# Expert loop of a decoder layer: the second layer's bias product reads 128 rows in place of three

## The chip, the cores and the metric

The kernel runs on one core of a Trainium2 chip. The metric is the device time of one execution in microseconds; the time given is the median of several runs. The engines of the core are named as the profile names them: PE is TensorE (PEld its weight loads), DVE is VectorE, ACT is ScalarE, POOL is GpSimd, SP is SyncE, which here only issues DMAs.

## What is computed

A decoder layer on x of 64 sequences x 64 tokens x 128 features: causal self-attention, cross-attention on a context, and a feed-forward layer with 8 experts of which each token takes 2. Each is followed by a residual sum and a layer norm. The change is in the experts:

```python
scores = x @ Wr.T + br                       # 8 experts
_, idx = top_k(scores + biases_N, 2)         # two experts per token
h = einsum('md,ndh->nmh', x, Wl1) + bl1      # first layer, 128 -> 512
a, b = h[..., :256], h[..., 256:]
y = einsum('nmh,nhd->nmd', silu(a) * b, Wl2) + bl2   # second layer, 256 -> 128
out = sum over the token's two experts of weight * y
```

The bias of the second layer, bl2 (8 x 128), is what the changed product adds.

## The kernel before

The 4096 tokens stand as 32 tiles of 128. The self-attention and the cross-attention are software pipelines over these tiles. In the cross-attention each group of four tiles is also routed: its tokens are sent by indirect DMA (`send`, POOL, L622) to per-expert regions of a DRAM buffer `xbuf`. The expert loop then works on 71 row tiles, each of 128 rows of one expert (`J` in the code). Its first tiles are interleaved with the last of the cross-attention; the last group is routed inside the loop.

Engines run their own instruction streams in a fixed order and meet by semaphores. `slot_tile(i, q)` is one step of the loop on each engine. On PE it does, in this order:

- `layer1(i)`: L1813, four fp32 products of 128 x 128 (two records each in the profile, so 8), `w_now` (the expert's first-layer weights) against the transposed rows `xT`
- `layer2(i - 2)`: L1823, two fp32 products (4 records), `gT` against `wl2_sb`, into columns 0 to 127 of a bank of PSUM, and then the bias product, L1825, which closes the same accumulation
- `x_T_slot(i + 2)`: L1803, the transposition of a coming row tile

SP fetches the rows (L443, 65 KB, from `xbuf`) and the weights (L448, 256 KB) four and three steps ahead; the fetch of weights waits until the first layer four tiles earlier is done. ACT copies the transposed rows (L878), copies and scales the result (L894) and applies silu (L886). DVE makes `gT` (L1440). POOL puts the result by indirect DMA into `zbuf` (`put`, L632).

The bias is added by PE. `b2_part` holds it split into three bf16 parts, one to a row (`split_b2`, DVE, six steps in the cross-attention); `ones_b`, a 128 x 128 matrix of ones in bf16, is the stationary operand, of which L1825 uses three rows. Summing the three rows gives the bias in every row of the result. The expert's number is read from a register (`bass.ds(e, 1)`), as for `wl2_sb`.

POOL writes the constants at the start (L479 to L521), some of them behind the first two tiles' L477, then issues five DMAs (L523 to L527), and next works on L533 of the first tile.

Of the kernel before, what the change touches and what calls it, by code (L numbers as in the profile page):

```python
# [25 lines left out]
BF16 = mybir.dt.bfloat16  # L26
# [5 lines left out]
P = 128  # L32
D = 128
# [10 lines left out]
def later(t, n):  # L44

    return t >= n if isinstance(t, int) else True


def decoder(nc, x, ctxT, g1, wqT, wkvT, woutT, g2, xwq, xwk, xwvT, xwo, bo, wrT, br, wl1, bl1, wl2, bl2, bN, out, xbuf, zbuf):
# [3 lines left out]
    NE = wrT.shape[1]  # L53
# [22 lines left out]
    with ctx:  # L76
        def sb(name, shape, dt=F32):
            return ctx.enter_context(nc.sbuf_tensor(name, shape, dt))
# [4 lines left out]
        bank = [ctx.enter_context(nc.psum_tensor(f"bank{i}", [P, 512], F32)) for i in range(8)]  # L83
# [34 lines left out]
        wl2_sb = sb("wl2_sb", [P, NE, NH, D])  # L118
        b2_sb = early[0:3, 0:W]
        b2_up = early[0:3, W:W + W // 2].bitcast(BF16)  # L120
        b2_part = sb("b2_part", [3, NE, D], BF16)
        part = sb("part", [3, 3])

        X = sb("X", [P, T, D])
# [44 lines left out]
        tri_b, ones_b = sb("tri_b", [P, P], BF16), sb("ones_b", [P, P], BF16)  # L169
# [169 lines left out]
        def numbers(eng_type, table, most, t, known):  # L339

            n = min(EB, J - t)
            _, values = nc.values_load_multi_w_load_instructions(
                table[0:1, t:t + n], engines=[eng_type], min_val=0, max_val=most,
                skip_runtime_bounds_check_because="an expert is a count of NE - 1 bounds, a row a block within the buckets")
            for k in range(n):
                known[t + k] = values[k]
# [63 lines left out]
        def _(sp):  # L410
# [5 lines left out]
            for n, (src, rows, _, _) in enumerate(slices):  # L416
                if n >= SELF_SPLITS:
                    sp.wait_ge(split, 2 * n)
                sp.dma_start(staging(n), src).then_inc(staged, 16)
                if n == 1:  # L420
                    sp.dma_start(wout_sb[:, :, :], woutT).then_inc(w_out, 16)
                    sp.dma_start(g2_sb[:, :], g2.partition_broadcast(P)).then_inc(w_out, 16)
                    sp.dma_start(X[:, 4:T, :], x_v[:, 4:T, :]).then_inc(x_rest, 16)
# [50 lines left out]
        def _(pool):  # L474
# [29 lines left out]
            ln_in(1, 1)  # L504
            nc.gpsimd.memset(tri_b[:, :], 1.0).then_inc(consts, 1)
            nc.gpsimd.memset(ones_b[:, :], 1.0)
            nc.gpsimd.memset(blank[:, 0:D], 0)
            nc.gpsimd.memset(blank[:, D + 1:ROW], 0)
            nc.gpsimd.memset(blank[:, D:D + 1], NOWHERE).then_inc(consts, 1)
# [408 lines left out]
        def _(dve):  # L918
# [5 lines left out]
            def split_slice(n):  # L924
                _, rows, hi, lo = slices[n]
                dve.wait_ge(staged, 16 * max(n + 1, SELF_SPLITS))
                V.tensor_copy(hi, staging(n)).then_inc(split, 1)
                dve.wait_ge(split, 2 * n + 1)
                V.tensor_tensor(lo, staging(n), hi.bitcast(F32), ALU.subtract).then_inc(split, 1)
# [213 lines left out]
            def cross(i, p):  # L1143
# [45 lines left out]
                if 2 <= i < 2 + 6:  # L1189
                    split_b2(i - 2)  # L1190
# [9 lines left out]
                            iota8[:, :].unsqueeze(1).broadcast_to([P, NE, NE]), ALU.is_ge)  # L1200

            def split_b2(n):
                out_of = b2_part[:, :, :].rearrange("r n d -> r (n d)")
                if n == 0:
                    dve.wait_ge(w_ffn, 80)
                    V.tensor_copy(b2_up[:, :], b2_sb[:, :]).then_inc(f["b2"], 1)
                if n == 1:
                    dve.wait_ge(f["b2"], 1)
                    V.tensor_scalar(out_of, b2_up[:, :], part[:, 0:1], None, ALU.mult).then_inc(f["b2"], 1)
                if n == 2:  # L1210
                    dve.wait_ge(f["b2"], 2)
                    V.tensor_tensor(b2_sb[:, :], b2_sb[:, :], b2_up[:, :], ALU.subtract).then_inc(f["b2"], 1)
                if n == 3:
                    dve.wait_ge(f["b2"], 3)
                    V.tensor_copy(b2_up[:, :], b2_sb[:, :]).then_inc(f["b2"], 1)
                if n == 4:
                    dve.wait_ge(f["b2"], 4)
                    V.scalar_tensor_tensor(out=out_of, in0=b2_up[:, :], scalar=part[:, 1:2], in1=out_of, op0=ALU.mult,
                                           op1=ALU.add)
                    V.tensor_tensor(b2_sb[:, :], b2_sb[:, :], b2_up[:, :], ALU.subtract).then_inc(f["b2"], 1)  # L1220
                if n == 5:
                    dve.wait_ge(f["b2"], 5)
                    V.scalar_tensor_tensor(out=out_of, in0=b2_sb[:, :], scalar=part[:, 2:3], in1=out_of, op0=ALU.mult,
                                           op1=ALU.add).then_inc(f["b2"], 1)
# [279 lines left out]
        def _(pe):  # L1504
            M = nc.tensor.matmul
# [311 lines left out]
            def layer2(t, q):  # L1817
                pe.wait_ge(hs["gT"], t + 1)
                if later(t, 2):
                    pe.wait_ge(hs["yb"], t - 1)  # L1820
                e = known[t]
                for c in range(NH):
                    M(bank[6 + q % 2][:, 0:D], gT[:, q % 2, c * P:(c + 1) * P],  # L1823
                          wl2_sb[:, bass.ds(e, 1), c, :].rearrange("h n d -> h (n d)"), start=(c == 0), stop=False)
                M(bank[6 + q % 2][:, 0:D], ones_b[0:3, :], b2_part[:, bass.ds(e, 1), :].rearrange("r n d -> r (n d)"),  # L1825
                  start=False, stop=True).then_inc(hs["L2"], 1)

            known = {}
# [1 line left out]
            def slot_tile(i, q):  # L1830
                of_tile(layer1, i, q, 0)
                if i == -1:
                    pe.wait_ge(f["tableA"], TABLE_A)
                if (i + 1) % EB == 0 and 0 <= i + 1 < J:
                    expert_numbers(mybir.EngineType.PE, i + 1, known)
                of_tile(layer2, i, q, 2)
                of_tile(x_T_slot, i, q, -2)
                if i == 4:
                    route_T(G - 1)
                if i == 6:  # L1840
                    route_scores(G - 1)
                if i == 12:
                    route_places(G - 1)
# [71 lines left out]
```

## Time and profile before

| | us |
|---|---|
| median of 3 runs (843.33 to 844.18) | 843.4 |
| span of the profiled execution | 876.8 |
| self-attention, cross-attention | 0 to about 692 |
| expert loop, first half (with sends) | about 692 to 782 |
| expert loop, second half | about 782 to 846 |
| last sums, layer norm, output | about 846 to 877 |

The profiled execution is 33.4 us longer than the median of the timed runs. Times below are from the start of its span. Over the whole span PE is busy 91%, its weight loads 75%, DVE 71%, ACT 68%, POOL 52%. A busy PE is not a PE at its peak, since its products overlap and their ends are modelled; what counts for pace is the distance between starts.

### The profile page before, as it was taken

What the parts mean: (1) busy time and instruction counts of PE and PEld (TensorE: products, weight loads), DVE (VectorE), ACT (ScalarE), POOL (GpSimd) and SP (SyncE); (2) the same over time, 40 slices, a digit from 0 to 9 for tenths busy, and PEclk for the clock granted to TensorE, in tenths of its full rate; (3) what the DMA queues carried; (4) which work ended last, traced back from release to release, by engine and by line L of the source; (5) the groups of instructions that cost most, each with busy time, mean ns of one, the idle gap of its engine ahead of it and who ended that gap; (6) DMA issues with size and microseconds to landing.
All of it is one profiled execution on the core that took longest, in us unless ns stands there. A gap on an engine that the chain in (4) does not pass through costs nothing.

```text
span 876.8 us, 26473 instructions
## 1 busy us (share of the span) xinstructions
PE 797.6 (91%) x9276; PEld 659.0 (75%) x9308; DVE 621.1 (71%) x1834; ACT 593.9 (68%) x1444; POOL 453.7 (52%) x441
## 2 busy tenths in 40 slices
PE   3799999999999988999999999999998979879996
PEld 2577787878777767887888888878786867768862
DVE  4877887878788757898787878878788534334425
ACT  2677888888788756677777767767675555446535
POOL 5477676776767732222535353535343455555543
PEclk9899999999999999999999999999999898999998
DMA  8499999000000000000000000000000445557636
GB/s 259 86 154 161 155 157 126 1 0 0 0 0 0 2 1 7 7 7 7 24 13 22 15 22 16 22 15 19 19 19 28 147 144 173 180 168 218 205 126 232
DMA packets 69392, 64.79 MB, mean 74 GB/s; under 512 B 5702, under 2 KB 54985, under 8 KB 69168
## 3 DMA queue, kind: packets, MB, share of 16 engines
q1 hardware_dynamic: 62592, 51.42, 29.0%
q0 software_dynamic: 4624, 9.61, 3.2%
q10 hardware_dynamic: 2080, 2.49, 0.9%
q8 instruction: 59, 0.97, 0.5%
q14 instruction: 37, 0.30, 0.1%
HBM read 35.37 MB, written 28.58 MB: 73 GB/s over the span
## 4 chain that ended last, share of the span: by engine, by line
PE 52%; issue 18%; POOL 12%; DVE 8%; ACT 5%; DMA 2%; another core or an unknown queue 2%; POOLq 0%; SPq 0%; ACTq 0%; DVEq 0%
PE bank L1813 8%; PE bank L1709 7%; PE bank L1509 5%; POOL rq L533 5%; PE bank L1511 5%; PE bank L1510 5%; PE bank L1823 3%; POOL PR L538 3%; PE bank L1684 3%; PE bank L1697 3%; PE bank L1585 2%; PE bank L1803 2%; PE bank L1593 2%; ACT VBD L393 2%
## 5 line engine op out<-in xcount | busy, mean ns | idle before, releaser
L393 ACT COPY VBD<-bank 64x512 f32<-64x512 f32 x192 | 111.3, 580 | 28.3 <-PE bank L1511 25.5
L570 POOL TENSOR_TENSOR PR<-PR,rL 128x1024 f32<-128x1024 f32 x32 | 60.9, 1904 | 115.0 <-DVE rL L1119 114.8
L533 POOL TENSOR_TENSOR rq<-ssq,mhalf 128x17 f32<-128x17 f32 x32 | 99.3, 3102 | 15.6 <-DVE ssq L968 15.1
L632 POOL DMA_INDIRECT zbuf<-PT,KT x71 | 69.7, 982 | 65.7 <-ACT PT L894 32.4
L538 POOL TENSOR_TENSOR PR<-PR,rL 128x1024 f32<-128x1024 f32 x32 | 61.0, 1906 | 82.4 <-DVE rL L999 82.4
L1440 DVE SCALAR_TENSOR_TENSOR stage<-bank,b_now,early 128x128 f32<-128x128 f32 x142 | 43.3, 347 | 77.1 <-ACT early L886 42.5
L1813 PE MATMUL bank<-xT,w_now 128*128 128x128 f32 x568 | 82.0, 291 | 1.1
L622 POOL DMA_INDIRECT xbuf<-xg,slot x64 | 65.2, 1018 | 34.1 <-DVE xg L1314 21.6
L886 ACT ACTIVATE early<-bank,b_now 128x128 f32<-128x128 f32 x142 | 44.7, 368 | 52.5 <-PE bank L1813 37.9
L1813 PEld LDWEIGHTS bank<-xT,w_now 128*128 128x128 f32 x568 | 77.1, 209 | 3.3 <-issue 3.2
L802 ACT ACTIVATE PT<-bank 128x512 f32<-128x512 f32 x64 | 38.3, 600 | 43.5 <-PE bank L1697 41.7
L1709 PE MATMUL bank<-VBD,PT 128*64 128x128 f32 x1024 | 64.7, 280 | 3.0 <-ACT PT L802 3.0
L1709 PEld LDWEIGHTS bank<-VBD,PT 128*64 128x64 f32 x1024 | 56.8, 139 | 11.6 <-ACT PT L802 9.5
L1593 PE MATMUL bank<-arena 128*128 128x128 f32 x512 | 62.8, 275 | 1.9 <-issue 1.1
L1585 PE MATMUL bank<-PT,VBD 128*128 128x512 f32 x128 | 63.4, 618 | 0.0
L1593 PEld LDWEIGHTS bank<-arena 128*128 128x128 f32 x512 | 59.8, 192 | 2.9 <-ACT arena L728 1.6
L1106 DVE TENSOR_REDUCE mx<-bank 128x8 f32<-128x512 f32 x64 | 43.8, 684 | 25.3 <-PE bank L1684 25.2
L575 POOL TENSOR_TENSOR rs<-ve,mhalf 128x1 f32<-128x1 f32 x32 | 18.6, 581 | 74.3 <-DVE ve L1134 73.9
L1509 PE MATMUL bank<-vo_lo,cT_hi 96*128 96x512 f32 x128 | 54.8, 428 | 2.4 <-DVE VBD L393 1.5
L712 ACT ACTIVATE PR<-bank 128x512 f32<-128x512 f32 x64 | 34.7, 595 | 28.9 <-PE bank L1563 28.9
L1511 PE MATMUL bank<-vo_hi,cT_hi 96*128 96x512 f32 x128 | 50.4, 394 | 0.0
L1510 PE MATMUL bank<-vo_hi,cT_lo 96*128 96x512 f32 x128 | 50.4, 393 | 0.0
(252 smaller groups left out, 2312.6 us busy)
## 6 DMA issues: line engine op xcount, KB each, us to landing
w_now<-in_wl SPq DMA_DIRECT2D x71, 256.0 KB
xbuf<-blank SPq DMA_DIRECT2D x1, 17160.0 KB, 119.6
KT<-xbuf SPq DMA_DIRECT2D x71, 65.0 KB
VBD<-zbuf SPq DMA_DIRECT2D x4, 512.0 KB, 5.0
out<-X SPq DMA_DIRECT2D x8, 256.0 KB, 2.3
cT<-in_ctxT ACTq DMA_DIRECT2D x16, 96.0 KB, 1.9
zbuf<-PT,KT POOLq DMA_INDIRECT x71
wl_sb<-in_wl POOLq DMA_DIRECT2D x1, 1024.0 KB, 9.2
```

Of the source, the lines that this page charges most:

```text
L393: u = copy(VBD[h * SEQ:(h + 1) * SEQ, p, s, lo:lo + blocks, :], bank[CHUNK_BANK[c]][s * SEQ:(s + 1) * SEQ, :].rearrange("k (a d) -> k a d" ...
L533: nc.gpsimd.tensor_tensor(rq[:, :], ssq[:, :], mhalf[:, 0:HEADS + 1], ALU.pow).then_inc(a["pow"], 1)
L538: nc.gpsimd.tensor_tensor(v, v, rL[:, p, :].unsqueeze(2).broadcast_to([P, HEADS, SEQ]), ALU.mult)\
L622: nc.gpsimd.indirect_dma_start(out=xbuf, out_offset=at, in_=xg[:, k, tt, :], in_offset=None)\
L632: nc.gpsimd.indirect_dma_start(out=zbuf, out_offset=at, in_=yb[:, t % YB, :], in_offset=None, bounds_check=K2 * TOK - 1, oob_is_err=False) ...
L1509: M(out_, l_hi, r_lo, start=True, stop=False)
L1510: M(out_, l_lo, r_hi, start=False, stop=False)
L1511: return M(out_, l_hi, r_hi, start=False, stop=True)
L1585: M(bank[4 + s][:, :], VBD[:, p, s, 0, :], PT[:, s * HW:(s + 1) * HW], start=True, stop=True)\
L1593: m = M(bank[0][:, 0:D], OT[:, k, :], wout_sb[:, k, :], start=(k == 0), stop=(k == NBLK - 1))
L1709: m = M(bank[bk][s * SEQ:(s + 1) * SEQ, 0:D], PT[:, k * P + s * SEQ:k * P + (s + 1) * SEQ], VBD[:, p, s, k, :], start=(k == 0), stop=(k == ...
L1813: m = M(bank[2 + q % 2][:, c * P:(c + 1) * P], w_now[:, q, c * P:(c + 1) * P], xT[:, q % 2, :], start=True, stop=True)
```

## The change

`b2_part` gets 128 rows in place of three. POOL fills it with zeros once among the constants, DVE writes the three parts into its first three rows as before, and the bias product reads all 128 rows of it and all 128 rows of `ones_b`. The tile has the same number of bytes in each partition as before. Lines behind L506 stand one lower in the changed kernel.

```diff
-        b2_part = sb("b2_part", [3, NE, D], BF16)
+        b2_part = sb("b2_part", [P, NE, D], BF16)
...
             nc.gpsimd.memset(ones_b[:, :], 1.0)
+            nc.gpsimd.memset(b2_part[:, :, :], 0.0)
             nc.gpsimd.memset(blank[:, 0:D], 0)
...
             def split_b2(n):
-                out_of = b2_part[:, :, :].rearrange("r n d -> r (n d)")
+                out_of = b2_part[0:3, :, :].rearrange("r n d -> r (n d)")
...
-                M(bank[6 + q % 2][:, 0:D], ones_b[0:3, :], b2_part[:, bass.ds(e, 1), :].rearrange("r n d -> r (n d)"),
+                M(bank[6 + q % 2][:, 0:D], ones_b[:, :], b2_part[:, bass.ds(e, 1), :].rearrange("r n d -> r (n d)"),
                   start=False, stop=True).then_inc(hs["L2"], 1)
```

## Rows read from the trace of the kernel before

**Rows 1.** The page's head: span and instructions.

```profile
span 876.8 us, 26473 instructions
```

**Rows 2.** Stretches: from:to, length, busy us (instructions) by engine, granted clock, DMA share, GB/s.

```profile
0.00:22.00 22.00, 7.92 (x46) 6.39 (x47) 9.32 (x25) 6.27 (x15) 12.60 (x37) 0.98 0.82 258
692.00:782.00 90.00, 73.59 (x508) 64.13 (x508) 35.34 (x155) 41.86 (x144) 48.49 (x51) 0.91 0.52 157
782.00:800.00 18.00, 18.00 (x144) 16.13 (x144) 7.98 (x31) 11.66 (x41) 9.28 (x10) 0.99 0.76 233
782.00:846.00 64.00, 62.24 (x485) 54.86 (x484) 27.33 (x103) 39.29 (x137) 33.69 (x35) 1.00 0.64 196
```

**Rows 3.** The chain of work that ended last, 692 to 847 us, shares by line.

```profile
by line: PE bank L1813 43.9%; PE bank L1823 17.2%; PE bank L1803 10.6%; another core or an unknown queue 8.4%; PE bank L1825 5.6%; issue 5.1%; ACT early L886 3.0%; DVE stage L1440 2.4%; ACT xT L878 1.3%; ACT PT L894 1.0%; POOL zbuf L632 0.6
```

**Rows 4.** Timeline of PE, 787.8 to 790.8 us: start, length, line, operands, rows*columns, count.

```profile
788.36 0.61 PE L1823 MATMUL bank<-wl_sb,stage 128*128 x4
788.90 0.23 PE L1825 MATMUL bank<-b_part,ones_b 3*128 x1
789.06 0.33 PE L1803 MATMUL bank<-ident,KT 128*128 128x128 f32 x1
789.23 1.06 PE L1813 MATMUL bank<-xT,w_now 128*128 128x128 f32 x8
790.12 0.61 PE L1823 MATMUL bank<-wl_sb,stage 128*128 x4
790.66 0.22 PE L1825 MATMUL bank<-b_part,ones_b 3*128 x1
```

**Rows 5.** Weight loads by line, 782 to 816 us: busy us, mean ns | idle before.

```profile
L1813 PEld LDWEIGHTS bank<-xT,w_now 128*128 128x128 f32 x152 | 19.8, 201 | 0.0
L1823 PEld LDWEIGHTS bank<-wl_sb,stage 128*128 128x128 f32 x76 | 10.0, 192 | 0.0
L1803 PEld LDWEIGHTS bank<-ident,KT 128*128 128x128 f32 x19 | 2.6, 139 | 1.5 <-issue 0.3
L1825 PEld LDWEIGHTS bank<-b_part,ones_b 3*128 3x128 bf16 x19 | 1.7, 91 | 2.3
```

**Rows 6.** Timeline of PE near 43 us: fp32 transpositions one behind another.

```profile
43.13 1.04 PE L1542 MATMUL bank<-ident,arena 128*128 128x128 f32 x8
44.00 0.27 PE L1548 MATMUL bank<-ident,kn 128*128 128x128 f32 x1
```

**Rows 7.** Timeline of weight loads near 46 us: fp32, then bf16.

```profile
46.01 0.86 PEld L1577 LDWEIGHTS bank<-ident,PR 128*128 128x128 f32 x8
46.83 0.21 PEld L1558 LDWEIGHTS bank<-causal,ident_b 128*128 128x128 bf16 x2
```

**Rows 8.** Timeline of weight loads near 392 us: the first of 64 rows.

```profile
391.97 0.15 PEld L1684 LDWEIGHTS bank<-KT,QT 64*64 64x64 f32 x4 [0.17 <-issue]
```

**Rows 9.** Timeline of PE near 415 us: short bf16 products of 128 rows.

```profile
414.94 0.22 PE L1739 MATMUL bank<-picked,ones_b 128*128 128x24 bf16 x3
415.02 0.18 PE L1741 MATMUL bank<-before,ones_b 128*128 128x32 bf16 x1
```

**Rows 10.** L1825 in 692 to 782, then 782 to 847 us: ns min/median/max, first and last start.

```profile
L1825 PE MATMUL bank<-b_part,ones_b x35: 224/225/283, 693.3 to 781.6; 3*128 x35
...
L1825 PE MATMUL bank<-b_part,ones_b x36: 224/225/225, 783.6 to 845.9; 3*128 x36
```

**Rows 11.** Timeline of POOL in the first 17 us.

```profile
1.12 0.53 POOL L482 MEMSET causal<- 128x512 bf16 x1
...
16.45 3.10 POOL L533 TENSOR_TENSOR rq<-ssq,mhalf 128x17 f32<-128x17 f32 x1 [4.47 <-DVE ssq L968]
```

**Rows 12.** POOL by line, 692 to 782 us; then what SP waited for, 782 to 846 us.

```profile
L632 POOL DMA_INDIRECT zbuf<-PT,KT x34 | 33.5, 986 | 34.5 <-ACT PT L894 22.5 <-issue 10.3 <-DVE xg L1314 1.6
L622 POOL DMA_INDIRECT xbuf<-xg,slot x15 | 14.8, 988 | 4.3 <-issue 4.3
...
SPq L448 <- PE bank L1813: 7.5, 16, 1.3
```

## The prediction

> **What bounds the kernel now.** I read the stages first, then the chain of work, then one tile at full pace, then its idle gaps. The expert loop does 71 row tiles (a row tile: 128 gathered tokens of one expert). It begins near 692 us and ends near 846 us of a span of 876.8 us [rows 1, 2]. In 782 to 846 us PE is busy 62.24 of 64 us, DVE 27.33, ACT 39.29, POOL 33.69, and the DMA engines 64% [rows 2]; in 782 to 800 us PE has no free time at all (18.00 of 18.00). The chain over the whole loop is mostly PE's: L1813, L1823, L1803 and L1825 (the changed product) together hold 43.9 + 17.2 + 10.6 + 5.6 = 77.3% [rows 3]. So a shorter PE tile should shorten the end. Before 782 us this is weaker: 35 products of L1825 take 90 us there, PE is busy 73.59 of it, and its granted clock averages 0.91.
>
> One tile at full pace is in [rows 4]: L1823 starts at 788.36, L1825 at 788.90, L1803 (the transposition of a coming tile's rows) at 789.06, L1813 (the first layer) at 789.23, and L1823 again at 790.12 us. That is a period of 1.76 us: 0.54 + 0.16 + 0.17 + 0.89. Eight products of L1813 take 0.89, so one fp32 step is 0.11. Three such steps are 0.33 of the 0.54, and the last step, from L1823 into L1825, is then **0.21, not 0.11**. Three of the fifteen steps stand out: into L1825 (0.21), out of it (0.16), and the one after L1803 (0.17).
>
> The weight loads show the same from the other side [rows 5]. In 34 us at full pace, loads of L1813 and L1823 have 0.0 us of idle ahead of them: each is made while the product before it still runs. The load of L1825 has 2.3 us over 19 (0.12 each) and that of L1803 1.5 us over 19 (0.08 each). These two are the ones at which the count of rows changes, from 128 to 3 and back to 128.
>
> **What the change does to a tile.** It replaces 71 products of 3 rows by 71 of 128 rows, in the same place, of the same 128 columns; the sum is the same, since the added rows are zero. No product is added, no wait is added or taken away.
>
> Is the number of rows what costs, or the bf16 type, or the register address of the expert? Other places tell. (a) A bf16 product of 128 rows right after fp32 products of 128 rows: the two loads of L1558 follow those of L1577 with no idle ahead of them; the last of L1577's begins near 46.87 - 0.14 = 46.73 (0.139 is the length of such a load in [rows 5]), L1558's first at 46.83, a normal step of 0.10 [rows 7]. Type alone costs nothing. (b) From fp32 products of 128 rows to fp32 products of 64 rows, no type change: L1684's load has 0.17 us of idle [rows 8]. Rows alone cost. (c) bf16 products of 128 rows and few columns follow each other at (415.02 - 414.94) / 3 = 0.03 us [rows 9]: such a load is short. (d) The register address is also on L1823, whose loads have no idle [rows 5].
>
> The Trainium skill says the same in "TensorEngine Tiling (Array Packing)", Key Properties: changing the tiling mode drains the engine, and a contraction over 32 rows or fewer is one of its row modes. It gives no figure; the sum does not use it.
>
> - Into L1825: 0.21 becomes one fp32 step, 0.11. **0.10 saved**; no lower end of the step below 0.11 is in sight, since the fp32 product before it must stream.
> - Out of L1825: 0.16. Its stream of 128 bf16 columns hides L1803's fp32 load or is hidden by it. The load paces at 0.11, as the transpositions of L1542 do: (44.00 - 43.13) / 8 = 0.109 [rows 6]; the floor is the short bf16 step of (c), 0.03. I take 0.11, the nearer row, since the next load is the same kind as L1542's. **0.05 saved** (ends 0 and 0.13).
> - After L1803: 0.17. The first load behind the switch is not hidden, so the next product is late; without the switch it is a step of L1542, 0.109. **0.06 saved** (ends 0 and 0.06).
>
> The sum is 0.10 + 0.05 + 0.06, with rounding of the rows about **0.20 us a tile**: 1.76 becomes 1.56. Ends: 0.10 if only the way in is gained, 0.29 if the way out falls to 0.03.
>
> **How many tiles gain.** After 782 us 36 of the products stand [rows 10] in 64 us: 1.78 each, practically all at PE's pace. They give 36 x 0.20 = 7.2 us. Before 782 us there are 35 [rows 10]; by the starts of L1825 in the timeline, from 693.3 to 781.6 us, 18 of their 34 intervals are 1.76; the rest end in waits on ACT, DVE or DMA that a faster PE does not shorten. They give 18 x 0.20 = 3.6 us. Together 10.8 us. If all 71 gain it is 14.2.
>
> What is late next in each part? Before 782 us it may be POOL: 34 puts (L632) and 15 sends (L622) there, each 0.99 us and, by L622's own row (4.3 us over 15), 0.29 of issue [rows 12]: 49 x 1.28 = 62.7 us, against 35 x 1.56 = 54.6 of PE. That holds the head's gain down to about what I count. After 782 us POOL has 35 x 1.28 = 45 us for 56. The DMA engines go from 76% at 233 GB/s (782 to 800 us) to 0.76 x 1.76 / 1.56 = 86%; the busiest stretch of the trace, the first 22 us, has 82% at 258 GB/s [rows 2]. This is close. SP still waits 7.5 us for L1813 in 782 to 846 us before it may fetch weights [rows 12], so these fetches are held by PE and not by bandwidth.
>
> **The rest.** One memset on POOL, of 128 x 1024 bf16. L482 writes half as much in 0.53 [rows 11], so it costs 1.0 us at about 7.5 us. POOL is then idle 4.47 us ahead of L533 at 16.45 us, and that idle covers it; the DMAs that POOL issues in between start 1 us later, all for data of later stages. Cost 0; uncovered it would be +1.0. DVE still writes three rows.
>
> **Own time.** The sum was made in an execution whose span, 876.8 us, is 33.4 us over the median of 843.4. Part of this must be waits that the timed runs don't have, and if they lie in the loop, more tiles run at PE's pace: that pulls towards 14.2. I take the count of the trace: 843.4 - 10.8 = **832.6 us**.
>
> **Rivals.**
> - **DMA or ACT takes over after 782 us.** With a period that can't fall below 1.66, the tail gives 3.6 and all gives 7.2: 836.2 us. For it: 86% DMA share. Against it: SP's waits for PE.
> - **Only the way in is gained** (the 0.16 and 0.17 belong to L1803's transposition): 54 x 0.10 = 5.4, 838.0 us. For it: L1803 is itself a different kind of step. Against it: L1542 is too, and runs at 0.109.
> - **Nothing is gained.** If a load can pass a running product only when it uses other rows of the array, a 128-row load behind a 128-row product has to wait as the 3-row load does, and the time stays at 843.4. Against it: loads of L1813 and L1823, all 128 rows behind 128 rows, have 0.0 idle [rows 5].
>  The Trainium skill states that rule ("TensorE: Matmul & The Clock Gate", Part 3, Measured speedup vs the span model: LDWEIGHTS overlaps an in-flight MATMUL only when its row group differs); the trace disagrees with it here.
> - **Slower.** The load of L1803 may no longer begin while L1825 runs. Now it begins 0.16 after L1825's start though that product lasts 0.23 (0.225) us [rows 4, 10], over 128 rows of which L1825 holds three. If a 128-row L1825 keeps those rows until its end, the way out goes from 0.16 to 0.23, and if the way in stays at 0.21, this is +0.07 x 71 = 5.0: 848.4 us. It decides from the point at which that load's wait costs more than the way in saves. Against it: bf16 products of 128 rows follow each other at 0.03 though each lasts 0.17 [rows 9].
>
> **How the numbers follow.** Forecast (0.20 a tile, 47 to 71 tiles, 829 to 834.5): 0.60. More than that (way out at 0.03): 0.05, down to 823 (71 x 0.29). DMA or ACT takes over: 0.12. Way in only: 0.09. Nothing: 0.10. Slower: 0.04. The range 829.0 to 839.0 holds the first and the two partial cases, 0.81, and leaves out the rest. A measurement of this kernel can tell about 0.2% from no change, 1.7 us. Faster by more: 0.60 + 0.05 + 0.12 + 0.09 = 0.86; within it 0.10; slower 0.04.
>
> **What would show it.** In the profile after: the load of L1825 (there L1826, one line lower) with no idle ahead of it, likewise L1803's; the period at 1.56 in the stretch that now has 1.76; PE's share of the chain still near 77%. The prediction is wrong if the period stays at 1.76 (nothing gained), if it is 1.66 (way in only), or if it falls to 1.56 in single tiles while new waits of PE for a DMA or for ACT stand between them. A granted clock below 0.91 over the first half of the loop would mean that PE's longer pauses cost back what its shorter tiles gave.

## The result

| | before | changed |
|---|---|---|
| median of 9 runs, us | 843.8 | 841.4 |
| lowest, highest | 841.7, 846.2 | 839.4, 843.1 |
| ratio, 95% interval | 1 | 0.9955 (0.9938 to 0.9972) |

The change makes the kernel faster by 0.45% (2.4 us by the medians, 3.8 by the ratio), where 10.8 us were forecast, and the time lies above the range of 829 to 839. The direction was right, and so was what the prediction said of PE's tile; two thirds of the forecast gain did not arrive (by the medians, more than three quarters).

PE's tile did become shorter, and by more than forecast. This is PE's timeline of the changed kernel in a stretch at full pace (start, length, line, operands, rows*columns, count; lines stand one lower than in [rows 4]):

```profile
764.43 0.61 PE L1824 MATMUL bank<-wl_sb,stage 128*128 x4
764.87 0.22 PE L1826 MATMUL bank<-b_part,ones_b 128*128 x1
764.93 0.28 PE L1804 MATMUL bank<-ident,KT 128*128 128x128 f32 x1
765.05 1.06 PE L1814 MATMUL bank<-xT,w_now 128*128 128x128 f32 x8
765.94 0.61 PE L1824 MATMUL bank<-wl_sb,stage 128*128 x4
```

The period is 765.94 - 764.43 = 1.51 us, where [rows 4] has 1.76. From L1824's start to the bias product: 0.44 (was 0.54), so that step is now 0.11. Out of the bias product: 0.06 (was 0.16). After the transposition: 0.12 (was 0.17). The sum of the three is 0.25 us a tile. The weight loads of the changed kernel in 765 to 808 us (the view of [rows 5]) show why:

```profile
L1814 PEld LDWEIGHTS bank<-xT,w_now 128*128 128x128 f32 x216 | 26.4, 192 | 1.1 <-ACT xT L879 1.1
L1824 PEld LDWEIGHTS bank<-wl_sb,stage 128*128 128x128 f32 x112 | 14.7, 192 | 0.5 <-issue 0.5
L1804 PEld LDWEIGHTS bank<-ident,KT 128*128 128x128 f32 x26 | 3.7, 142 | 0.3
L1826 PEld LDWEIGHTS bank<-b_part,ones_b 128*128 128x128 bf16 x27 | 2.7, 100 | 0.0
```

The load of the bias product has no idle ahead of it any more (2.3 us over 19 before) and the transposition's 0.3 over 26 (1.5 over 19). At 0.25 a tile, 71 tiles would give 17 us. So the question is where most of it went.

One thing has to be put right first. The execution of the kernel before on which the prediction rests had a span of 876.8 us, 33 above the median. The profiled execution of the changed kernel has a span of 840.2 (841.96 us in all), and another of the kernel before, from the first experiment, has 845.3. Comparisons below use these two. In the one of 845.3 the 71 bias products take 126.4 us, in place of 152.6 in the one that the prediction read: the many waits before 782 us belong to that one execution and not to the kernel.

### The profile page after: what moved, and what is told of

Same layout as the page of the kernel before. It is cut to its first block, busy times and chain, and to the rows that moved or that the text cites. A ratio compares the mean times of both kernels' runs of the same rounds, so it can differ in the third digit from the quotient of the medians.

```text
span 840.2 us, 26506 instructions
## 1 busy us (share of the span) xinstructions
PE 773.7 (92%) x9308; PEld 648.0 (77%) x9308; DVE 620.4 (74%) x1834; ACT 596.3 (71%) x1444; POOL 453.9 (54%) x442
## 4 chain that ended last, share of the span: by engine, by line
PE 40%; issue 22%; POOL 17%; DVE 9%; ACT 6%; DMA 4%; SPq 1%; POOLq 0%; ACTq 0%; DVEq 0%
POOL rq L534 7%; PE bank L1710 6%; PE bank L1814 5%; PE bank L1510 5%; PE bank L1512 4%; PE bank L1511 4%; POOL PR L539 3%; PE bank L1824 2%; PE bank L1698 2%; ACT VBD L393 2%; PE bank L1685 2%; POOL rs L548 2%; POOL rs L544 2%; POOL rs L477 2%; PE bank L1586 1%
## 5 line engine op out<-in xcount | busy, mean ns | idle before, releaser
L534 POOL TENSOR_TENSOR rq<-ssq,mhalf 128x17 f32<-128x17 f32 x32 | 99.2, 3101 | 16.9 <-DVE ssq L969 16.4
L623 POOL DMA_INDIRECT xbuf<-xg,slot x64 | 64.8, 1012 | 34.0 <-DVE xg L1315 21.4
L1814 PE MATMUL bank<-xT,w_now 128*128 128x128 f32 x568 | 78.1, 282 | 4.1 <-DMA w_now<-in_wl 2.7
L1814 PEld LDWEIGHTS bank<-xT,w_now 128*128 128x128 f32 x568 | 71.0, 196 | 6.0 <-ACT xT L879 3.2
L969 DVE TENSOR_REDUCE ssq<-arena 128x17 f32<-128x1088 f32 x32 | 41.2, 1288 | 12.9 <-ACT arena L677 5.2
```

Source lines behind the costliest of these rows:

```text
L534: nc.gpsimd.tensor_tensor(rq[:, :], ssq[:, :], mhalf[:, 0:HEADS + 1], ALU.pow).then_inc(a["pow"], 1)
L623: nc.gpsimd.indirect_dma_start(out=xbuf, out_offset=at, in_=xg[:, k, tt, :], in_offset=None)\
L1814: m = M(bank[2 + q % 2][:, c * P:(c + 1) * P], w_now[:, q, c * P:(c + 1) * P], xT[:, q % 2, :], start=True, stop=True)
```

## The experiments

All tables below count from the start of the loop's first bias product, and call the loop what lies between it and the last bias product, since the loop's own start moves by some 5 us from one execution to the next (682 to 688 us). The last send is the start of POOL's last L622 (L623). "Fetch of tile 40" is the DMA of the rows of row tile 40 (L443; tiles are counted from 0). It is the first tile that depends on the last group's routing: SP issues its fetch only when all sends have landed (L435).

### 1. The kernel before and the changed one again

> The kernel before, unchanged, for an execution whose span is near its timed median. Theory Q (the queue of POOL caps the first half of the expert loop): SP fetches the rows of tile 40 (L443 behind L435) only after POOL's last send, and POOL's indirect DMAs stand 1.28 us apart with no wait for the last ten or so before it; that fetch is issued about as long after the loop's first product of L1825 as in the changed kernel, where it is 750.97 - 686.31 = 64.7 us, within 1 us. Rival P (PE sets the first half as well): it is issued about 40 x 0.245 = 8 to 10 us later relative to that product, 73 to 75 us. Period of a tile at full pace 1.757 us in both.

> The changed kernel, unchanged. Period at full pace 1.512 us (steps of 0.112, 0.056 and 0.117 around the changed product). Theory Q: 3 to 5 us faster than the kernel before, all of it from tile 40 on; the fetch of tile 40's rows 64 to 66 us after the loop's first bias product. Rival P: the same total would have to come evenly from both halves.

| from the first bias product, us | before | changed, two executions |
|---|---|---|
| last send | 61.3 | 61.0, 61.0 |
| fetch of tile 40 | 65.0 | 64.7, 64.7 |
| bias product of tile 40 | 75.5 | 77.1, 77.3 |
| last bias product | 126.4 | 123.0, 123.2 |

The repeated kernel before came out at a ratio of 0.9990 (0.9972 to 1.0009), the changed one at 0.9941 (0.9918 to 0.9964). The last send and the fetch stand at the same time in both, within 0.4 us, though PE's tile differs by 0.25 us. Nothing PE gains in the first 40 tiles gets past this point. Of the 3.2 to 3.4 us that the loop gains, all comes after it: from tile 40's product to the end 50.9 us become 45.9, while that product itself comes 1.6 us later.

What holds the sends is POOL's own queue. POOL by line in the 65 us up to the fetch (count, busy us, mean ns, idle before), first of the kernel before, then of the changed one:

```profile
L632 POOL DMA_INDIRECT zbuf<-PT,KT x34 | 33.6, 987 | 11.4 <-issue 8.2 <-ACT PT L894 2.7 <-DVE xg L1314 0.5
L622 POOL DMA_INDIRECT xbuf<-xg,slot x14 | 13.9, 993 | 4.2 <-issue 2.7 <-ACT PT L894 1.4
```

```profile
L633 POOL DMA_INDIRECT zbuf<-PT,KT x34 | 33.7, 991 | 11.1 <-issue 7.9 <-ACT PT L895 3.2
L623 POOL DMA_INDIRECT xbuf<-xg,slot x14 | 13.7, 977 | 4.2 <-issue 3.5 <-ACT PT L895 0.6
```

48 indirect DMAs, nearly each with the 0.30 us of issue between it and the next. That is a chain of 1.285 us each: the timeline of POOL in the changed kernel around the last send reads

```profile
742.14 0.98 POOL L633 DMA_INDIRECT zbuf<-PT,KT  x1 [0.30 <-issue]
743.43 0.97 POOL L623 DMA_INDIRECT xbuf<-xg,slot  x1 [0.31 <-ACT PT L895]
744.71 0.99 POOL L633 DMA_INDIRECT zbuf<-PT,KT  x1 [0.30 <-ACT PT L895]
746.00 0.98 POOL L633 DMA_INDIRECT zbuf<-PT,KT  x1 [0.30 <-issue]
747.28 0.97 POOL L623 DMA_INDIRECT xbuf<-xg,slot  x1 [0.30 <-issue]
```

and PE of the same execution, behind it:

```profile
749.76 0.22 PE L1826 MATMUL bank<-b_part,ones_b 128*128 x1
752.84 0.33 PE L1804 MATMUL bank<-ident,KT 128*128 128x128 f32 x1 [2.86 <-DMA KT<-xbuf]
754.67 2.04 PE L1814 MATMUL bank<-xT,w_now 128*128 128x128 f32 x8 [1.50 <-DMA w_now<-in_wl]
756.50 1.06 PE L1824 MATMUL bank<-wl_sb,stage 128*128 x4
757.36 0.31 PE L1826 MATMUL bank<-b_part,ones_b 128*128 x1
```

PE runs dry for 2.9 us until the rows have landed and for 1.5 more until the weights of tile 39 have, which stand behind them in SP's queue. The eight products of L1814 then last 2.04 us in place of 1.06. The granted clock is 1.00 over the 65 us before, and behind the pause it is at the lower of its two levels (1.2 GHz) for 6.5 us. Two stretches of the changed kernel, then the one behind the pause of the kernel before (the view of [rows 2]; the clock is the third number from the end):

```profile
753.70:760.20 6.50, 5.53 (x26) 5.48 (x27) 0.78 (x3) 1.77 (x7) 1.95 (x2) 0.50 0.80 251
760.20:763.40 3.20, 3.20 (x31) 3.14 (x29) 1.56 (x6) 2.04 (x9) 0.98 (x2) 0.96 0.57 164
```

```profile
756.50:763.30 6.80, 6.75 (x54) 6.13 (x54) 2.34 (x9) 3.81 (x14) 2.82 (x3) 1.00 0.88 279
```

The kernel before has the same place with a shorter pause, and no slow products behind it:

```profile
753.86 0.23 PE L1825 MATMUL bank<-b_part,ones_b 3*128 x1
754.72 0.33 PE L1803 MATMUL bank<-ident,KT 128*128 128x128 f32 x1 [0.63 <-DMA KT<-xbuf]
756.54 1.13 PE L1813 MATMUL bank<-xT,w_now 128*128 128x128 f32 x8 [1.50 <-DMA w_now<-in_wl]
757.51 0.61 PE L1823 MATMUL bank<-wl_sb,stage 128*128 x4
```

This spell is the whole reason why tile 40's product comes later. Counted from the first bias product, L1814 starts again at 68.4 us (754.67 - 686.31), 0.3 us before the kernel before does (756.54 - 687.85 = 68.7), and the fetch of the rows is 3.7 us ahead of it in both. From there to the bias product of tile 40 the changed kernel takes 8.7 us and the kernel before 6.8. At the higher level it would be about 5.9 (1.4 to the next bias product and three periods of 1.51, an estimate from the timelines here), so the lower clock costs some 2.7 us.

The two stretches side by side (the view of [rows 2]: PE, PEld, DVE, ACT, POOL, clock, DMA share, GB/s), before and changed:

```profile
688.00:753.00 65.00, 64.21 (x516) 57.40 (x516) 36.72 (x159) 44.80 (x149) 47.51 (x50) 1.00 0.71 216
753.00:815.00 62.00, 59.78 (x469) 52.69 (x468) 25.69 (x99) 38.93 (x133) 34.23 (x35) 1.00 0.66 204
```

```profile
686.00:751.00 65.00, 59.47 (x528) 56.65 (x526) 37.67 (x162) 45.86 (x152) 47.97 (x50) 1.00 0.72 217
751.00:810.00 59.00, 54.24 (x459) 52.62 (x460) 24.90 (x95) 37.72 (x130) 34.19 (x35) 0.94 0.70 214
```

In the kernel before PE is busy 64.21 of 65 us, and POOL's 48 x 1.285 = 61.7 us of queue fill nearly all of them as well: two limits at nearly the same height. The page of POOL alone would not say so (47.51 busy of 65 is 73%); the 0.30 of issue between two of its DMAs is not counted as busy.

### 2. What makes the step long: 64 rows, 96 rows, two switches more

```diff
-        b2_part = sb("b2_part", [P, NE, D], BF16)
+        b2_part = sb("b2_part", [DH, NE, D], BF16)
...
-                M(bank[6 + q % 2][:, 0:D], ones_b[:, :], b2_part[:, bass.ds(e, 1), :]...
+                M(bank[6 + q % 2][:, 0:D], ones_b[0:DH, :], b2_part[:, bass.ds(e, 1), :]...
```

DH is 64; with 96 in its place it is the second kernel.

> The bias product over 64 rows (3 used, 61 zero) in place of 128. If it is the switch between the row modes that costs, and not the small number of rows as such, 64 rows cost as much as three: steps into and out of the product 0.207 and 0.156 us, period 1.757 us, time equal to the kernel before within 0.3%. If only the sizes below 33 rows cost, period 1.512 us and the time of the changed kernel.

> The bias product over 96 rows. The cross-attention's products of 96 rows follow those of 128 without the extra tenth of a microsecond, those of 64 rows with it. If 96 counts as the full mode, the steps are 0.112 and 0.056 us and the period 1.512 us, as with 128; else 0.207, 0.156 and 1.757, as with 3 and with 64.

PE's timeline with 64 rows:

```profile
770.69 0.61 PE L1824 MATMUL bank<-wl_sb,stage 128*128 x4
771.24 0.23 PE L1826 MATMUL bank<-b_part,ones_b 64*128 x1
771.39 0.33 PE L1804 MATMUL bank<-ident,KT 128*128 128x128 f32 x1
771.56 1.06 PE L1814 MATMUL bank<-xT,w_now 128*128 128x128 f32 x8
772.45 0.61 PE L1824 MATMUL bank<-wl_sb,stage 128*128 x4
```

and with 96:

```profile
775.65 0.61 PE L1824 MATMUL bank<-wl_sb,stage 128*128 x4
776.10 0.22 PE L1826 MATMUL bank<-b_part,ones_b 96*128 x1
776.16 0.28 PE L1804 MATMUL bank<-ident,KT 128*128 128x128 f32 x1
776.27 1.06 PE L1814 MATMUL bank<-xT,w_now 128*128 128x128 f32 x8
777.17 0.39 PE L1824 MATMUL bank<-wl_sb,stage 128*128 x2
```

With 64 rows a tile takes 1.76 us and the kernel is at 0.9997 (0.9977 to 1.0017) of the kernel before; with 96 it takes 1.52, and the one run gave 839.7 us. Their loops agree with this: 127.0 us with 64 rows (126.4 before), 123.3 with 96 (123.0 and 123.2 in the changed kernel). So it is not the number of rows as such: 64 costs what 3 costs, 96 what 128 costs. In this chain of 128-row products, a product of 3 or of 64 rows is a change of row mode, twice.

The other way round, the kernel before gets a second 3-row product, of zeros, between the two fp32 products of the second layer:

```diff
+        none_b = sb("none_b", [3, D], BF16)
...
+            nc.gpsimd.memset(none_b[:, :], 0.0)
...
+                    if c == 0:
+                        M(bank[6 + q % 2][:, 0:D], ones_b[0:3, :], none_b[:, :], start=False, stop=False)
```

> The kernel before with one more 3-row bf16 product (of zeros, so the sum is the same) between the two fp32 products of the second layer: two more switches for each of the 71 tiles. Period at full pace 1.757 + 0.25 to 0.31 = 2.01 to 2.07 us. Theory Q (POOL caps the first 40 tiles at about 64.7 us): PE's 40 x 2.04 = 82 us now passes POOL's, so the whole 71 x 0.28 = 20 us less the slack that the kernel before has in the first half (0 to 10 us) appears: 10 to 20 us slower. Rival P: 71 x 0.28 = 20 us slower, no less. If waits of another kind set the loop: under 5 us slower.

```profile
791.24 0.39 PE L1825 MATMUL bank<-wl_sb,stage 128*128 x2
791.56 0.22 PE L1828 MATMUL bank<-none_b,ones_b 3*128 3x128 bf16 x1
791.72 0.49 PE L1825 MATMUL bank<-wl_sb,stage 128*128 x2
792.14 0.23 PE L1829 MATMUL bank<-b_part,ones_b 3*128 x1
792.29 0.33 PE L1805 MATMUL bank<-ident,KT 128*128 128x128 f32 x1
```

The period is 2.11 us, 0.35 more than before, above the 0.25 to 0.31 expected (the product itself is in it too, and it stands between two fp32 products). The time went to 863.1 us, a ratio of 1.0228 (1.0202 to 1.0255), +19.3 us. 71 x 0.35 would be 25; the loop grew by 21.0, from 126.4 to 147.4. Here PE has overtaken POOL: the last send is at 70.2 us in place of 61.3, the fetch of tile 40 at 73.9 in place of 65.0, the stall there is gone, and most of the price is paid. A tile that is 0.35 us longer thus costs 21.0 of 25 us, and one that is 0.245 us shorter gives 3.4 of 17. Two limits of nearly equal height do that. By itself this run does not show it: 19.3 us also lies near the 20 us that its rival (PE alone sets the pace) gave with a step of 0.28.

### 3. Sends earlier

The eight sends of the last group stand in POOL's order at steps 16 to 34. They are moved forward, with the same work done:

```diff
-        LAST_SENDS = {16: 0, 19: 1, 22: 2, 24: 3, 27: 4, 30: 5, 32: 6, 34: 7}
+        LAST_SENDS = {16: 0, 17: 1, 19: 2, 20: 3, 22: 4, 23: 5, 25: 6, 26: 7}
```

> The changed kernel with the eight sends of the last group in steps 16, 17, 19, 20, 22, 23, 25, 26 of POOL's loop in place of 16, 19, 22, 24, 27, 30, 32, 34. Nothing else moves; the same work is done. Theory Q (in the changed kernel PE's gain of the first half ends in the wait for POOL's last send): eight puts less stand ahead of that send, it is issued 8 x 1.285 = 10 us earlier, at 50.7 in place of 61.0 us after the first bias product, and the stall of 7 + 1.4 us at tiles 37 and 38 is gone or moved to where the result buffers run full: 833 to 836 us, the loop 115 to 119 us in place of 123. Rival D (the fetch of weights or DMA bandwidth holds the first half): no change, 839 to 841 us.

> The kernel before with the same earlier sends. Theory Q: it has only one stall there, of 2.4 us at tile 37; it gains 1 to 3 us (841 to 843), so that the bias product's change is then worth 7 to 10 us (theory Q) in place of 4. Rival D: no change in either, and the difference between the two kernels stays 4.

| us | before | before, early sends | changed | changed, early sends |
|---|---|---|---|---|
| last send | 61.3 | 51.0 | 61.0 | 50.9 |
| fetch of tile 40 | 65.0 | 63.6 | 64.7 | 63.3 |
| bias product of tile 40 | 75.5 | 74.3 | 77.1 | 73.3 |
| last bias product | 126.4 | 125.2 | 123.0 | 119.6 |
| ratio to before | 1 | 0.9990 (0.9973 to 1.0008) | 0.9941 to 0.9955 | 0.9895 (0.9875 to 0.9914) |

With the early sends the bias product's change is worth 0.95% (0.9990 to 0.9895, some 8 us; 6.8 by these runs' medians), with the late ones 0.45 to 0.59%; in the loop it is 5.6 us (125.2 to 119.6) in place of 3.2 to 3.4. In the kernel before they give nothing measurable (1 to 3 us were expected, 0.8 is what the ratio says, and it is within its interval). So part of the lost gain was indeed in the wait for the last send, and most of that part was the clock: from 65 us behind the first bias product to the loop's end the granted clock averages 1.00, where it is 0.94 in the changed kernel (751 to 810 us), and tile 40's product comes 3.8 us earlier though its fetch comes 1.4 us earlier. The fetch did not move by 10 us: SP now waits in front of it for puts. It fetches the rows of tile t only when the result of tile t - 12 has been put (L337), and the puts stand in the same queue, now behind the sends. Within the loop these waits are 15.3 us over 18 with the early sends, 11.3 over 14 in the changed kernel, and 1.0 over 2 in the kernel before (9.9 over 3, of which 8.9 is one wait at the loop's end). The loop took 119.6 us where 115 to 119 was expected, and the time 838.4 where 833 to 836 was. That the length of POOL's queue holds the rest is what the next experiment bears on.

### 4. POOL's queue longer

To separate the queue's length from its order, 31 short operations are put behind the puts of the changed kernel:

```diff
+        more = sb("more", [P, 32])
...
                 of_tile(put, i, q, 3)
+                if 3 <= i < 34:
+                    nc.gpsimd.tensor_tensor(more[:, i - 3:i - 2], mhalf[:, 0:1], mhalf[:, 1:2], ALU.pow)
```

> The changed kernel with one more operation of one column (a power, about 0.57 us as the two of L477) behind each of 31 puts on POOL, in steps 3 to 33; nothing reads it. Theory Q (POOL has no free time in the first half): every one of them delays the last send, 31 x 0.57 = 17.7 us, so the fetch of tile 40's rows goes from 64.7 to 82 us after the first bias product and the time from about 840 to 856 to 858. Rival (POOL only happens to be busy, its buffers of eight results give slack): 0 to 5 us.

POOL's timeline in this kernel, 754 to 758 us:

```profile
754.79 1.03 POOL L634 DMA_INDIRECT zbuf<-PT,KT  x1 [0.18 <-issue]
755.86 0.59 POOL L640 TENSOR_TENSOR more<-mhalf 128x1 f32<-128x1 f32 x1
756.62 1.02 POOL L624 DMA_INDIRECT xbuf<-xg,slot  x1 [0.18 <-issue]
757.95 0.99 POOL L634 DMA_INDIRECT zbuf<-PT,KT  x1 [0.30 <-issue]
```

The last send went from 61.0 to 76.6 us, the fetch of tile 40 from 64.7 to 80.3, and the last bias product from 123.0 to 137.3. The time is 856.4 us, a ratio of 1.0128 (1.0103 to 1.0153), some 15 us above the changed kernel. Of 31 x 0.57 = 17.7 us of added work on an engine that the page calls 54% busy, 15.6 appear at the last send. The gaps explain the rest: by the timeline there are 0.04 and 0.18 us around the added operation in place of one gap of 0.30, and 31 x 0.08 is 2.5. In the changed kernel POOL has no free time in this half.

### 5. The order of SP's two fetches

```diff
-                of_tile(load_rows, i, q, -4)
                 of_tile(load_weights, i, q, -3)
+                of_tile(load_rows, i, q, -4)
```

> The changed kernel with the order of the two fetches in a step of SP's loop exchanged: the weights of tile i + 3 before the rows of tile i + 4. At tile 40 the fetch of the rows waits for the last send, and with it now also the weights of tile 39 behind it, 0.53 us later; they land 3.0 us after that, and PE restarts 3.7 us after the fetch of the rows. With the weights first PE can restart when the rows have landed, 1.9 us after their fetch: 1.8 us faster if the queue's order costs that, 0 if the rows of tile 40 are the later of the two or the weights' fetch then delays the rows elsewhere.

The ratio is 0.9938 (0.9917 to 0.9960), not told apart from the changed kernel's. In the profiled execution the bias product of tile 40 comes at 73.6 us in place of 77.1 and the last one at 119.8 in place of 123.0, more than the 1.8 expected. PE's L1814 starts again 1.9 us earlier (66.5 us in place of 68.4), as expected, and the lower clock lasts 3.4 us there (751.6 to 755.0 us) in place of 6.5, which is most of the rest. One execution and the ratio don't agree on the size of the gain, and I leave it open.

### 6. The memset alone

The kernel before with the 128-row tile and its memset, but the product over three rows:

```diff
+            nc.gpsimd.memset(b2_part[:, :, :], 0.0)
...
-                M(bank[6 + q % 2][:, 0:D], ones_b[0:3, :], b2_part[:, bass.ds(e, 1), :]...
+                M(bank[6 + q % 2][:, 0:D], ones_b[0:3, :], b2_part[0:3, bass.ds(e, 1), :]...
```

> The kernel before with the 128-row tile and its memset on POOL, but the product still over three rows. The memset takes 1.0 us in the idle of POOL ahead of L533: time equal to the kernel before within 0.2%. If it moves the start of the self-attention, +1.0 us; if a later start of the DMAs behind it helps, up to 1 us less.

0.9990 (0.9971 to 1.0009): nothing. The changed kernel's timeline of POOL has it at 0.96 us, and L534 where it was, with the idle ahead of it shorter ([rows 11] has 16.45 and 4.47):

```profile
7.35 0.96 POOL L507 MEMSET b_part<- 128x1024 bf16 x1
...
16.44 3.10 POOL L534 TENSOR_TENSOR rq<-ssq,mhalf 128x17 f32<-128x17 f32 x1 [3.78 <-DVE ssq L969]
```

### 7. Both together

The changed kernel with the weights fetched first, and the last sends either as in experiment 3 or at every second step from 16 to 30:

> The changed kernel with both the earlier sends and the weights fetched ahead of the rows. The earlier sends alone were 0.9895 of the kernel before, the other order of fetches alone 0.9938 against 0.9941 to 0.9955 of the changed kernel. If the order matters only where the fetch of rows waits for the last send, the two together give no more than the sends alone, 0.989; if it also helps where the rows wait for a put twelve tiles back, 1 to 2 us more, 0.987 to 0.988.

> As the last, with the eight sends in every second step from 16 to 30. POOL's total is the same. If what is left of the first half is POOL's total (puts and sends, 1.285 us each, 58 us to the last send), the time is that of the earlier sends within 0.2%, 0.987 to 0.990; if it is the wait of the row fetch for the last send, it lies between them and the changed kernel, 0.991 to 0.993.

| | ratio to before | median, us | last send | fetch of tile 40 | last bias product |
|---|---|---|---|---|---|
| early sends, weights first | 0.9914 (0.9883 to 0.9945) | 836.9 | 50.0 | 63.0 | 117.9 |
| every second step, weights first | 0.9868 (0.9838 to 0.9898) | 835.9 | 55.1 | 62.2 | 118.9 |

The times of the first scatter from 834.7 to 844.5. Its interval overlaps the second's and that of the early sends alone, so the three can't be ranked. All are faster than the kernel before; the second, like the early sends alone, is also below the changed kernel's intervals. The first was expected at 0.987 to 0.989, and at 0.9914 its middle misses this. That the sends at 55 us are no worse than at 50 fits the length of POOL's queue as what is left; it does not prove it.

## Why the prediction was wrong

**Mechanism in PE's tile.** Right. The bias product's number of rows was the cost, the type and the register were not, and full rows removed it. The rival "nothing gained", with the rule that a load passes a running product only over other rows, fell: 128-row loads behind 128-row products have 0.0 us of idle. So did the rival "slower": the load of L1804 does start while the bias product runs. "Way in only" fell too. One of the four reasons was weaker than it was put, though. Under (b), the loads of L1684 are 64*64, so their columns change too, and in the same stretch a load at which only the columns change has the same idle:

```profile
390.63 0.58 PEld L1709 LDWEIGHTS bank<-VBD,PT 128*64 128x64 f32 x10
391.38 0.42 PEld L1718 LDWEIGHTS bank<-ident,X 128*128 128x128 f32 x4 [0.17 <-issue]
```

That rows alone cost is shown by the runs with 64 and 96 rows, not by [rows 8].

**Size of the step.** Too small: 0.20 forecast, 0.245 measured. The term is the way out. I took 0.11 for it, as if the transposition's load had to pace it, and it is 0.056, between that and the 0.03 of [rows 9], whose products have only 24 and 32 columns. What sets it is not shown. Into the product 0.10 forecast and 0.095 measured, after the transposition 0.06 and 0.05.

**Number of tiles that gain.** This is the step that failed. For the head (the loop's part with the sends) the prediction had POOL's 62.7 us of puts and sends beside PE's, and wrote that this "holds the head's gain down to about what I count", 3.6 us. It compared the 62.7 with the new PE time (54.6) and not with the old one: 35 x 1.76 = 61.6. POOL's 62.7 was no lower than what PE had already, so the head could give nothing; only the 90 us that the head took in that one execution made room for a gain. It gave 0.3 us up to the fetch of tile 40, and minus 1.6 at the product of tile 40. The rival that "DMA or ACT takes over" was set after 782 us; it is POOL, and before it.

**What comes behind the wait.** The tail (36 tiles) was forecast to give 7.2. From tile 40 on (30 intervals) it gave 5.0, in spite of the larger step: at full pace it would be 44.0 us long (27 x 1.512, and 3.2 for the last three intervals), and 1.9 of waits, most of them between tiles 44 and 45 and between 60 and 61, make it 45.9. And 1.6 was paid ahead of it, which no step of the prediction held: a PE that arrives early at the wait stands dry for longer, and has the lower clock behind it, some 2.7 us. The 3.7 us from the fetch of the rows to PE's start are the same in both kernels. The prediction's last sentence names the clock over the first half and longer pauses; no price was put on it, and over the first 65 us the clock was 1.00, the spell came behind them. 5.0 - 1.6 = 3.4 us is what the loop gained (126.4 to 123.0).

**The trace it rests on.** The prediction counted 18 head intervals at full pace from an execution 33 us longer than the median. In the execution near the median 31 of the first 36 intervals are at pace (PE busy 64.21 of 65 us). The longer one made the head look like a place of scattered waits, and hid that two engines are at their limit there together. I noted the 33 us and concluded that the gain might be larger; it was the reverse. In that execution PE waits 13.4 us for ACT's copies of the rows (L878) before 782 us, in the other 0.7, and the DMA engines move 157 GB/s there in place of 213; what made them slower is open. One end of the prediction's range is also a little off: 47 tiles of 0.20 give 834.0 us, not 834.5.

**Left over.** By the ratios the kernel gained 3.8 to 5.0 us, by the loop 3.2 to 3.4. The loop starts between 682 and 688 us in all these executions, of either kernel, so that single profiles can't say whether the rest is real. Whether the DMA engines, 70 to 72% busy, limit anything here is not shown by any run.

## What to carry to other kernels

In a chain of full matmuls, one product over 3 or over 64 rows costs 0.25 us more here than the same product padded with zero rows; look for it in the idle ahead of weight loads, where the number of rows changes. Before a saving on the busiest engine is counted, add up for every other engine the distance from one start to the next of its queued work, not its busy time: a POOL that was "73% busy" was full. And compare that sum with the old time of the stretch, since a second limit at the same height takes the whole gain, and the wait that then appears has a price of its own: here a lower clock behind it.

## What the runs showed that I had not expected

- 96 rows count as the full mode (period 1.51 to 1.52 us), 64 as the small one (1.76).
- Out of a full-mode bf16 product of 128 columns into an fp32 load the step is 0.056 us, half an fp32 step, although that fp32 load by itself paces at 0.11.
- The Trainium skill's page "TensorEngine Tiling (Array Packing)", Key Properties, has a change of tiling mode drain the engine. The runs agree that the change costs time, though not that the engine is empty in between (L1803 starts 0.16 us after L1825, which lasts 0.23 by its modelled end), and give the price in this kernel: 0.095 us on the way in, 0.10 on the way out and 0.05 at the next product.
- With the shorter tile and the sends at their old place, PE waits 2.9 to 7.5 us for the rows of tile 40, and products at the lower clock follow, in all five profiled executions (the changed kernel twice, 96 rows, weights first, the longer POOL queue). With the product of 3 or 64 rows the wait is 0.6 to 0.7 us in three (the kernel before again, 64 rows, the memset alone), and no slow products follow.
- An indirect DMA of 128 rows holds POOL's queue for 1.285 us, of which 0.30 counts as idle; with a short operation between two of them, the gap is 0.18 [the timeline of experiment 4].
